# Router statistics two steps later, and keys group N1 ahead of score group S1, in an attention step order written out by hand

## The reference, cut to what matters

```
x = x + 0.5 * moe(layernorm(x), Wg, w1, w2)        # 8 experts, top 2, capacity 320
x = x + attention(layernorm(x), w_qkv, w_o)        # 16 heads of 16, causal softmax
x = x + 0.5 * moe(layernorm(x), Wg, w1, w2)
```

```
scores = einsum('bhqd,bhkd->bhqk', q, k) / sqrt(16), masked causally
probs  = softmax(scores);  attn = einsum('bhqk,bhkd->bhqd', probs, v)
x      = x + attn @ w_o.T
```

## Time and profile before

| | us |
|---|---|
| median of three runs | 798.94 (796.29 to 802.18) |
| the profiled execution | 800.13 |
| its span, first to last instruction | 798.4 |
| PE busy in the span | 759.0 (95%) |
| DVE busy | 420.7 (53%) |
| ACT busy | 374.7 (47%) |
| POOL busy | 326.2 (41%) |

### The profile page before, as it was taken

The page is one execution under the profiler, slowest core; times in us unless marked ns, Lnnn a source line. Parts: engine busy times, 40 slices in busy tenths (PEclk is TensorE's granted clock), DMA queues, the critical chain, the costliest instruction groups (busy, mean ns, idle before and its releaser), DMA issues. The chain is left out here.

```text
span 798.4 us, 16072 instructions
## 1 busy us (share of the span) xinstructions
PE 759.0 (95%) x6248; PEld 672.1 (84%) x6248; DVE 420.7 (53%) x738; ACT 374.7 (47%) x630; POOL 326.2 (41%) x384
## 2 busy tenths in 40 slices
PE   8979999999999999898998989979999999999997
PEld 5879999999999986565665665757999999999997
DVE  4854634634544238767677576346544544634630
ACT  4535534544544211655645556632544634634631
POOL 7274454455424264141231122244463363464133
PEclk9999999999999999999999999989999999999999
DMA  9565255255232154211222020043553364264012
GB/s 307 179 195 134 48 159 130 45 155 132 68 95 28 21 166 158 82 40 48 81 83 95 21 79 30 28 144 79 174 151 97 84 160 117 56 162 130 9 24 26
DMA packets 61863, 80.28 MB, mean 101 GB/s; under 512 B 10916, under 2 KB 48804, under 8 KB 61812
## 3 DMA queue, kind: packets, MB, share of 16 engines
q1 hardware_dynamic: 46452, 60.34, 22.5%
q0 software_dynamic: 15360, 19.23, 13.1%
HBM read 49.62 MB, written 19.01 MB: 86 GB/s over the span
## 5 line engine op out<-in xcount | busy, mean ns | idle before, releaser
L687 DVE SCALAR_TENSOR_TENSOR second_h_lo<-second_ps_h,second_h_hi 128x320 fp32r<-128x320 f32 x128 | 63.0, 492 | 103.2 <-ACT second_h_hi L535 103.2
L687 DVE SCALAR_TENSOR_TENSOR first_h_lo<-first_ps_h,first_h_hi 128x320 fp32r<-128x320 f32 x128 | 63.0, 492 | 103.2 <-ACT first_h_hi L535 103.2
L438 POOL DMA_INDIRECT after_first<-first_scaled,first_add_now x40 | 69.4, 1735 | 113.1 <-ACT first_scaled L528 106.4
L438 POOL DMA_INDIRECT out_dram<-second_scaled,second_add_now x40 | 69.0, 1724 | 113.1 <-ACT second_scaled L528 107.9
L1253 DVE TENSOR_REDUCE at_maxima<-at_ps_front 128x4 f32<-128x512 f32 (+2 forms) x96 | 97.0, 1040 | 21.2 <-PE at_ps_front L1397 20.9
L1100 POOL TENSOR_SCALAR_AFFINE_SELECT at_probs<-at_probs 128x512 f32<-128x512 f32 x64 | 41.4, 659 | 160.2 <-ACT at_probs L1167 160.2
L810 PE MATMUL second_ps_o<-second_w_hi,second_h_hi 128*128 128x256 f32 x320 | 90.7, 284 | 0.0
L810 PE MATMUL first_ps_o<-first_w_hi,first_h_hi 128*128 128x256 f32 x320 | 90.7, 284 | 0.0
L1167 ACT ACTIVATE at_probs<-at_ps_keys 128x768 f32<-128x768 f32 (+1 forms) x96 | 81.1, 880 | 18.4 <-PE at_ps_keys L1428 18.2
L810 PE MATMUL second_ps_o<-second_w_lo,second_h_hi 128*128 128x256 f32 x320 | 89.5, 280 | 0.0
L810 PE MATMUL first_ps_o<-first_w_lo,first_h_hi 128*128 128x256 f32 x320 | 89.5, 280 | 0.0
(11 more groups left out here) (295 smaller groups left out, 1742.4 us busy)
## 6 DMA issues: line engine op xcount, KB each, us to landing
first_w_raw<-in_L_ffn_w_dram SPq DMA_DIRECT2D x16, 1024.0 KB, 8.8
second_w_raw<-in_L_ffn_w_dram SPq DMA_DIRECT2D x15, 1024.0 KB, 6.9
at_q_stack<-at_pre_hi SPq DMA_DIRECT2D x12, 256.0 KB, 2.5
at_k_stack<-at_pre_hi SPq DMA_DIRECT2D x12, 256.0 KB, 2.6
x<-_attn_hidden_states_dram SPq DMA_DIRECT2D x4, 512.0 KB, 5.7
after_first<-x SPq DMA_DIRECT2D x4, 512.0 KB, 6.8
normed_rows<-first_xn SPq DMA_DIRECT2D x4, 512.0 KB, 3.3
x<-after_first SPq DMA_DIRECT2D x4, 512.0 KB, 6.1
```

What stands on the lines that cost most here:

```text
L438: pool.indirect_dma_start(sum_rows, bass.IndirectOffsetOnAxis(ap=add_now[par][:, s:s + 1], axis=0), scaled[par][:, s, :], None, bounds_che ...
L687: v.scalar_tensor_tensor(h_lo[:, f, a * HALF:(a + 1) * HALF], ps_h[:, f % 2, a, 0:HALF], 0.0, h_hi[:, f, a * HALF:(a + 1) * HALF].bitcast( ...
```

## The change

Two edits to the order. In steps 0 to 13, N[1] stands ahead of S[1] instead of behind it. And the statistics of batches 0 and 1 are cut out of project(b) into an item of their own, "moments", which stands in steps 9 and 13 behind S[5] and ahead of the work item; batches 2 and 3 take their statistics inside project as before. Only DVE has work in the new item; it signals nothing to another engine. No instruction is added, removed or changed otherwise.

```
+        moments = [("moments", (v - 9) // PER_BATCH)] if v in (9, 13) else []
...
-        return (N[0] + S[0] + S[1] + N[1] + S[2] + N[2] + S[3] + N[3] + normal + turns + N[4] + S[4] + project +
-                outputs + S[5] + work + N[5])
+        return (N[0] + S[0] + N[1] + S[1] + S[2] + N[2] + S[3] + N[3] + normal + turns + N[4] + S[4] + project +
+                outputs + S[5] + moments + work + N[5])
...
                 v_.wait_ge(front_v, FRONT_V[FRONT_AT[item]])
                 v_.sem_inc(out_ready, 1)
+                if b >= BATCH - 2:
+                    added_moments(b)
+
+            def added_moments(b):
+
                 for t in range(QT * b, QT * (b + 1)):
                     last = v_.bn_stats(stats[:, t, :], x[:, t, :])
                 chain(last)
                 for t in range(QT * b, QT * (b + 1)):
                     v_.bn_aggr(router.moments[:, t, :], stats[:, t, :])
```

More of the change, by code:

```diff
@@ L1314, in _ @@
                 what, of = item[0], item[1:]
-                if what in ("statistics", "normalize", "rows", "stacks", "scores", "turns", "outputs", "project", "logits", "weights"):
-                    {"statistics": statistics, "normalize": normalize, "rows": rows, "stacks": stacks, "scores": scores, "turns": turns,
+                if what in ("statistics", "normalize", "rows", "stacks", "scores", "turns", "outputs", "project", "logits", "weights", "moments"):
+                    {"moments": added_moments, "statistics": statistics, "normalize": normalize, "rows": rows, "stacks": stacks, "scores": scores, "turns": turns,
                      "outputs": outputs, "project": project, "logits": logits, "weights": weights}[what](*of)
@@ L1493, in _ @@
                 what, of = item[0], item[1:]
-                if what not in ("statistics", "normalize", "weights", "next_rows"):
+                if what not in ("statistics", "normalize", "weights", "next_rows", "moments"):
                     {"rows": rows, "stacks": stacks, "values_in": values_in, "scores": scores, "turns": turns,
```

## The result

| | before | after |
|---|---|---|
| median, us (10 runs each) | 799.47 (796.29 to 802.18) | 803.83 (802.10 to 804.84) |
| profiled execution, us | 800.13 | 804.66 |
| its span, us | 798.4 | 802.9 |
| its mean granted clock | 0.987 | 0.983 |

The ratio is 1.0055, with a 95% interval of 1.0034 to 1.0076: the change costs 4.4 us, 0.55%. The forecast was +2.9, that is 801.8, with a range of 797 to 806. The measured 803.83 lies inside that range, and just above the 800.0 to 803.3 that the sum's own bounds gave. First PE's waits from 322 to 497 us in the kernel after (us in total, times, the longest); they answer to the earlier trace rows.

What follows compares the result with a forecast made beforehand. PE bounds the kernel, and S1, its reduction and S3 set a step's length. Swap +0.9 and +2.9, statistics -0.9: +2.9 us on the median 798.94 gives 801.8, own range 800.0 to 803.3, wider range 797 to 806.

Steps and rivals of the forecast that it cites:

- The swap after a values item: Steps 2, 6 and 10: N1 waits for ACT's exponential of N5, making S1 and S3 0.96 us late; 2.9 us in all.
- One sign: Steps after a values item: PE's wait ahead of S3 stays about as long as before the change.
- The swap after a stacks item: Steps 1, 3, 5, 7, 9, 11: S1, its reduction and S3 each 0.15 us late; 0.9 us in all.
- After rows items: Steps 0, 4 and 8: N1 fits into the wait ahead of S1, and nothing is gained or lost: 0.
- Steps 12 and 13: No work item before them and DVE behind with its reductions, so N1's place doesn't matter: 0.
- The statistics: Leaving DVE's queue in steps 7 and 11, they free steps 8 and 12 by 0.43 us each; 0.9 us gained.
- Their new place: Behind S5 in steps 9 and 13: 1.8 us of statistics fit DVE's idle 2.39 and 2.31 us, cost 0.
- The sum: Whole kernel: 0.9 + 2.9 - 0.9 = +2.9 us, with bounds of +1.1 to +4.4.
- The first: Rival, chance 0.15: the clock also falls in steps 2, 6 and 10, 1.6 us each, giving 806.6 us.
- The second: Rival, chance 0.15: moved statistics keep the clock up in steps 8 and 12, 1.6 us each, giving 798.6 us.
- The third rival: Chance 0.10: N1 fills the wait ahead of S1, nine steps gain 0.26 us each, giving 795.7 us.
- a changed number of stretches at half clock: Sign against the forecast: more or fewer stretches with PE's granted clock at 0.50, the 1.2 GHz level.

## Why the prediction was right

**The swap after a values item, right.** Predicted 0.96 us a step; 0.89, 0.92 and, up to S3, 0.87 measured. S1 came 0.98 late, as worked out; S3 only 0.87. The missing 0.11 is S1 itself: before, it was the first work behind a wait and its reduction began 0.78 us after its start (393.82 to 394.60), now 0.67 (397.34 to 398.01). The experiment with N5 early shows the cause, and that with half of the reduction shows why nothing absorbs it. One sign went otherwise: PE was to wait about as long as before ahead of S3, but in step 6 the row of S3 shows no wait before and 0.88 us after: N1 and its wait, which had stood between S1 and S3, now stand in front of S1.

**The swap after a stacks item, right in kind, mis-sized.** Predicted 0.15 a step, measured 0.05 to 0.08. S1 is 0.17 late, much as worked out, but the same quicker S1 gives 0.11 of it back and S3 is only 0.06 late: what failed is the step "so S3 is 0.15 us late as well". The six steps cost 0.34 us and not 0.9. After rows items 0.00 and -0.03 against 0, as predicted. Steps 12 and 13 were not lengthened by the swap: where it stands alone, S3 of both starts as before.

**The statistics, right in kind, a little too high.** Predicted 0.43 twice; 0.37 at S0 of step 8, and for step 11 0.39 where the statistics move alone (0.43 in the kernel after). The 0.17 that step 12 loses again is missing in the sum, so 0.6 and not 0.9 is left. The reciprocal of step 7 began as soon as PE's last outputs matmul was done, which is the bound that the sum used. Their new place cost nothing, and moving them to where DVE isn't idle cost 2.4.

**The sum, right at an equal clock**: +2.9 predicted, +2.9 ± 0.6 worked out from the runs. That the digits agree is luck: the terms read from the steps are 0.3, 2.7 and -0.6, some 2.4 together, where 0.9, 2.9 and -0.9 were predicted, and the errors of the first and the third go against each other. What the sum lacked is the clock: the medians differ by 4.4, and only the wider range held the measured time.

**The rivals.** The first (the clock falls in steps 2, 6 and 10 too) came true in one step of three in the profiled execution. The second (it stays up in steps 8 and 12) came true in step 8 alone: that step is 1.94 us shorter, of which 0.37 are the statistics and the rest the clock, as the price of 1.6 had it. In step 12 the clock fell before and after (0.85 and 0.86 over the step). And the statistics needn't be the reason: in the profiles of the three kernels that only swap, with the statistics in their old place, the clock fell in neither step, and with N5 early, where the statistics are moved, it fell in step 8. The third rival fell: in step 5 the wait ahead of S3 grew (0.70 to 0.81) instead of shrinking by what N1 filled. The prediction also named a changed number of stretches at half clock as a sign of being wrong. In steps 0 to 13 there are two in either profile, in other places; over the whole span six before and eight after, and the two more stand at 11.6 us and at the span's end.

Whether the swap lowers the clock isn't shown. For it: in the twelve profiles a fall begins in steps 2, 6 or 10 three times in the nine such steps in which the swap makes S1 wait for N5's exponential (once in the kernel after, twice with the swap alone, not at all with the swap only there), and not once in the other 27. Against it: the kernels with N5 early or with S1 ahead in all steps, which don't have its long waits, ran at 0.9851 and 0.9861, and the statistics alone at 0.9873. Why some of these orders run at a lower mean clock than others stays open.

## What to carry to other kernels

Before work is moved into a wait, look up when its own release comes: if it comes no earlier than the one being waited for, the move puts the second wait in front of the first. Then ask what the stretch is worth: work taken out of a stretch that another engine's chain sets gives nothing, and the same work put in front of that chain's start delays the chain, together with what that work waits for (0.06 us a step here after stacks items, some 0.9 after values items), unless it fits wholly into a wait there (after rows items, 0). What gains is to start the chain earlier, as with S1 ahead of S0, and the gain ends at the next wait, which has to be named too.

## What the runs showed of the hardware

In these profiles a group of matmuls that is the first behind a wait takes about 0.11 us longer until its reader can start: S1 with its eight matmuls 0.78 us behind a wait, 0.67 us right behind N1. And the granted clock fell in places where no wait of PE's matmuls was longer than 0.95 us (step 8 before, step 10 after): behind 1.77 us of busy PE in 3.40 it fell in step 10 of the kernel after and not in step 6, though both have the same work and the same waits. Mean clocks between 0.979 and 0.995 of single executions go with times that differ by up to 8 us (0.016 x 520), more than the change itself.
